# The causal convolution of a Mamba block moved from VectorE to TensorE, in an eight-core Mamba + mixture-of-experts kernel

## What is computed

```python
xn = layernorm(x)
# Mamba branch
z, xBC, dt = split(xn @ in_proj_w)            # 2048 | 2304 | 32
y_conv = conv_b                               # causal depthwise convolution, 4 taps
for k in range(4):
    y_conv = y_conv + xp[:, k:k+L, :] * conv_w[3 - k]
xBC = silu(y_conv)                            # x_part 2048 | B 128 | C 128
state = state * decay + (x_t * dt_t) outer B_t   # scan over tokens, 32 heads of 64
y = state . C_t + x_part * D
g = rmsnorm(y * silu(z)) * norm_w
att = g @ out_proj_w
# MoE branch, every expert computed for every token
ffn = sum_e w_full[:, e] * (xn @ expert_w[e].T)    # 8 experts, top-2 weights
out = x + att + ffn
```

## Time and profile before

| | us |
|---|---|
| median of 2 runs | 1998.78 (1997.82 to 1999.73) |
| the profiled execution | 2002.32 |
| its span (slowest core, core 2) | 2000.8 |
| spans of the eight cores | 1982.9 to 2000.8 |

### The profile page before, as it was taken

How to read it: one execution, slowest core, us unless ns; L and a number is a source line. 1 busy time by engine, 2 the same in 40 slices (tenths; PEclk the granted TensorE clock), 3 DMA queues, 4 the chain that set the end, 5 groups by cost and what they waited for, 6 DMA issues and landing times.

```text
span 2000.8 us, 23963 instructions; the slowest of 8 cores (1982.9 to 2000.8 us)
## 1 busy us (share of the span) xinstructions
PE 1090.3 (54%) x7419; PEld 748.8 (37%) x7419; DVE 1062.4 (53%) x2347; ACT 402.4 (20%) x483; POOL 0.2 (0%) x4
## 2 busy tenths in 40 slices
PE   1111246485757475657665666665576558573400
PEld 1110233363445344544444444543363346342100
DVE  3642474638353845476547645664556454745344
ACT  2354102120122022102220132112111221022200
POOL 0000000000000000000000000000000000000000
PEclk9999988795878688879787887888786779686755
DMA  6852000000000100000010000000100000000077
GB/s 165 283 179 74 27 22 19 22 30 22 22 27 22 45 27 27 22 24 27 27 43 24 30 22 25 25 27 22 48 25 24 19 25 28 27 11 22 11 245 259
DMA packets 64930, 103.62 MB, mean 52 GB/s; under 512 B 8870, under 2 KB 49958, under 8 KB 62246
## 3 DMA queue, kind: packets, MB, share of 16 engines
q1 hardware_dynamic: 60198, 89.51, 14.3%
q10 hardware_dynamic: 4608, 12.58, 1.6%
HBM read 85.28 MB, written 16.78 MB: 51 GB/s over the span
## 4 chain that ended last, share of the span: by engine, by line
PE 35%; DVE 25%; DVEq 9%; issue 8%; ACT 7%; DMA 3%; SPq 1%; ACTq 0%
PE P L639 12%; DVEq L72 8%; PE P L736 6%; PE P L787 6%; PE P L1070 6%; DVE AC L764 6%; DMA OACR<-oaccd 2%; DVE SCR L1017 2%; DVE Y L1012 2%; DVE OACC L660 2%; DVE AC L758 2%; ACT TX L834 2%; DVE AC L845 1%; DVE Y L1023 1%; ACT TZ L799 1%
## 5 line engine op out<-in xcount | busy, mean ns | idle before, releaser
L639 PE MATMUL P<-EWB,XN 128*128 128x256 bf16 x4096 | 581.5, 304 | 195.5 <-DVE EWB L610 108.4
L639 PEld LDWEIGHTS P<-EWB,XN 128*128 128x128 bf16 x4096 | 436.8, 108 | 333.4 <-issue 228.3
L660 DVE SCALAR_TENSOR_TENSOR OACC<-P,WFULL,OACC 128x256 bf16<-128x256 f32 x448 | 213.6, 481 | 376.5 <-PE P L639 356.5
L787 PE MATMUL P<-WIN,XN 128*128 128x512 bf16 x512 | 148.3, 456 | 72.1 <-DVE SZ L822 72.1
L736 PE MATMUL P<-XN,WIN 128*128 128x256 bf16 x1152 | 133.9, 275 | 55.0 <-DVE XB L578 41.1
L764 DVE SCALAR_TENSOR_TENSOR AC<-XB,CW,AC 128x256 bf16<-128x256 bf16 x288 | 139.6, 485 | 22.5 <-issue 1.3
L736 PEld LDWEIGHTS P<-XN,WIN 128*128 128x128 bf16 x1152 | 112.1, 98 | 73.7 <-issue 59.9
L1052 PE MATMUL P<-IBF,Y 128*128 128x128 bf16 x256 | 29.0, 304 | 190.3 <-DVE Y L1026 161.4
L1070 PE MATMUL P<-WOUT,SCR 128*128 128x512 bf16 x512 | 120.9, 397 | 9.2 <-ACT SCR L1059 6.7
L1059 ACT COPY SCR<-P 128x2048 bf16<-128x2048 bf16 x16 | 29.8, 1865 | 465.6 <-PE P L1052 465.6
L787 PEld LDWEIGHTS P<-WIN,XN 128*128 128x128 bf16 x512 | 56.3, 113 | 156.0 <-issue 121.4
(11 more groups left out here) (121 smaller groups left out, 999.1 us busy)
## 6 DMA issues: line engine op xcount, KB each, us to landing
ESTG<-we SPq DMA_DIRECT2D x256, 128.0 KB, 2.1
XR<-x SPq DMA_DIRECT2D x32, 512.0 KB, 5.9
WSTG<-wi SPq DMA_DIRECT2D x8, 1098.0 KB, 7.2
WSTG<-wi SPq DMA_DIRECT2D x8, 1078.0 KB, 8.5
WOSTG<-wo SPq DMA_DIRECT2D x16, 512.0 KB, 4.3
out<-OST ACTq DMA_DIRECT2D x16, 512.0 KB, 5.7
attd<-ATTS ACTq DMA_DIRECT2D x16, 256.0 KB, 2.0
oaccd<-OACC SPq DMA_DIRECT2D x4, 1024.0 KB, 4.5
```

Of the source, the lines that this page charges most:

```text
L639: li = e.matmul(pp4[:, of4:of4 + 256], XN[:, k * L + t * 128:k * L + (t + 1) * 128], EWB[:, eb * 2048 + k * 256:eb * 2048 + (k + 1) * 256] ...
L660: return e.scalar_tensor_tensor(OACC[:, t * 256:(t + 1) * 256], pp4[:, of4:of4 + 256], WFULL[:, t * 8 + ee:t * 8 + ee + 1], OACC[:, t * 25 ...
L787: li = e.matmul(P01[:, bb * 512:(bb + 1) * 512], XN[:, k * L + ch * 128:k * L + (ch + 1) * 128], WIN[:, k * WIN_F + w * 1024 + bb * 512: k ...
```

## The change

- Convolution. Each of the 18 tiles is now four accumulating matmuls of 128x256 on PE. The moving operand is XB shifted by 0 to 3 columns; the weights are four 128x128 diagonal matrices that hold the tap's coefficients. ACT makes the diagonals for every tile anew, by four ACTIVATEs of the identity matrix IBF with a per-partition scale, into a ring of eight (DGS, two tiles). Even tiles accumulate in the second bank of P01, odd tiles in the second bank of P67.
- The result leaves PSUM through ACT: once with the bias to AC, once through tanh with half the bias (CBH, a new constant) to TX. DVE does the two remaining SiLU instructions after every second tile. The separate SiLU waves after the z steps are gone.
- The xBC projections come in nine waves of two tiles, in the first bank of P01. The z steps and the transposes into P01 are halved in width too, so there are twice as many of them.
- The MoE groups rotate over three banks instead of four.
- State update: DVE adds straight from PSUM (P23); YIN and its two ACT copies a chunk are gone. The second half's matmuls wait for the first half's addition.
- The numbers of MoE steps per place (drip) are set anew: 204 in a pair and its two backs, 202 before.

The core of the diff:

```diff
@@ mcbh = st("V", lambda e: e.tensor_scalar_mul(CBH[:], CB[:], 0.5), ...)   (new, once)
-                            sl4 = gi % 4
+                            sl4 = gi % 3
-                            of4 = (sl4 % 2) * 512
+                            of4 = (sl4 % 2) * 512 if sl4 < 2 else 0
-                            if gi >= 4:
-                                ww.append(escq[gi - 4])
+                            if gi >= 3:
+                                ww.append(escq[gi - 3])
...
-                        for wv, (ct0, ctn) in enumerate(
-                                [(0, 4), (4, 4), (8, 4), (12, 4), (16, 2)]):
+                        for wv in range(9):
+                            ct0 = 2 * wv
...
-                            drip(4)
+                            drip(2)
...
+                        cv_ev = [None, None]
+                        mm_cv = {}
...
+                            def dgen(e, ct=ct):
+                                for dd in range(4):
+                                    j = (4 * ct + dd) % 8
+                                    li = e.activation(
+                                        DGS[:, j * 128:(j + 1) * 128],
+                                        IBF[:], AF.Identity,
+                                        scale=CW[:, ct * 4 + dd:ct * 4 + dd + 1])
+                                return li
+                            mdg = st("S", dgen, waits=[mm_cv.get(ct - 2)])
+                            yield
+                            cvp, cvo = (P01, 512) if ct % 2 == 0 else (P67, 512)
+                            def cvmm(e, ct=ct, cvp=cvp, cvo=cvo):
+                                for dd in range(4):
+                                    j = (4 * ct + dd) % 8
+                                    li = e.matmul(
+                                        cvp[:, cvo:cvo + 256],
+                                        DGS[:, j * 128:(j + 1) * 128],
+                                        XB[:, ct * XBW + 4 - dd:
+                                           ct * XBW + 260 - dd],
+                                        start=(dd == 0), stop=(dd == 3))
+                                return li
+                            mm_cv[ct] = st("T", cvmm, waits=[
+                                mdg, wave_ev[ct // 2], cv_ev[ct % 2]])
                             drip(3)
                             yield
+                            def cvev(e, ct=ct, cvp=cvp, cvo=cvo):
+                                e.activation(
+                                    AC[:, ct * 256:(ct + 1) * 256],
+                                    cvp[:, cvo:cvo + 256], AF.Identity,
+                                    scale=1.0, bias=CB[:, ct:ct + 1])
+                                e.drain()
+                                return e.activation(
+                                    TX[:, (ct % 2) * 256:(ct % 2 + 1) * 256],
+                                    cvp[:, cvo:cvo + 256], AF.Tanh, scale=0.5,
+                                    bias=CBH[:, ct:ct + 1])
+                            cv_ev[ct % 2] = st("S", cvev, waits=[
+                                mm_cv[ct], cms.get(ct - 2)])
+                            yield
+                            if ct % 2 == 1:
+                                def comp(e, ct=ct):
+                                    e.tensor_scalar(TX[:], TX[:], 0.5, 0.5,
+                                                    ALU.mult, ALU.add)
+                                    e.drain()
+                                    return e.tensor_tensor(
+                                        AC[:, (ct - 1) * 256:(ct + 1) * 256],
+                                        AC[:, (ct - 1) * 256:(ct + 1) * 256],
+                                        TX[:], ALU.mult)
+                                cm = st("V", comp,
+                                        waits=[cv_ev[0], cv_ev[1]])
+                                cms[ct] = cms[ct - 1] = cm
+                                drip(2)
+                                yield
...
-                        msu = st("T", supd, waits=[st_c23[0], mx])
-                        drip(3)
+                        msu = st("T", supd, waits=[st_c23[0], mx] +
+                                 ([msup] if msup else []))
+                        drip(2)
                         yield
-                        ev = st("S", lambda e, w=w: e.copy(
-                            YIN[:, w * 1024:(w + 1) * 1024], P23[:]),
-                            waits=[msu])
+                        md = st("V", lambda e, c=c, w=w, dto=dto:
+                                e.tensor_tensor(
+                            hx(DTX[:, dto + w * 1024:dto + (w + 1) * 1024], 16),
+                            hx(S_ALL[:, w * 1024:(w + 1) * 1024], 16),
+                            BETB[:, c * 32 + w * 16:c * 32 + (w + 1) * 16]
+                            .to_broadcast([128, 16, HEADDIM]),
+                            ALU.mult), waits=[msu])
+                        drip(1)
+                        yield
+                        msup = st("V", lambda e, w=w, dto=dto: e.tensor_tensor(
+                            S_ALL[:, w * 1024:(w + 1) * 1024],
+                            DTX[:, dto + w * 1024:dto + (w + 1) * 1024],
+                            P23[:], ALU.add), waits=[md], drain=False)
```

More of the change, by code:

```diff
@@ L138, in build_nc @@
         CB = E(nc.sbuf_tensor([128, NXT], F32))
+        CBH = E(nc.sbuf_tensor([128, NXT], F32))
         KCOL = E(nc.sbuf_tensor([128, 2], F32))
@@ L205, in build_nc @@
             ][-1])
+            mcbh = st("V", lambda e: e.tensor_scalar_mul(
+                CBH[:], CB[:], 0.5), waits=[mconst])
             ma1 = st("S", lambda e: e.activation(ROWA[:], ROWA[:], AF.Exp),
@@ L752, in front_gen @@
                             yield
-                        mcv_tiles = []
+                        cv_ev = [None, None]
+                        mm_cv = {}
+                        cm = None
+                        cms = {}
                         for ct in range(NXT):
[L755 to L775, removed]
@@ L792, in zmm @@
                                                 start=(k == 0), stop=(k == NK - 1))
[L793 to L810, removed]
+                                        return li
+                                    mz = st("T", zmm,
+                                            waits=[st_c01[0], m_szprev[0]])
+                                    drip(2)
@@ new lines, in front_gen, with zef @@
+                                    yield
+                                    def zef(e, ch=ch, w=w, bb=bb):
+                                        e.activation(
+                                            TZ[:, bb * 512:(bb + 1) * 512],
+                                            P01[:, 0:512], AF.Tanh, scale=0.5)
+                                        e.drain()
+                                        return e.copy(
+                                            SZ[:, (ch % 2) * D_INNER + w * 1024 + bb * 512:
+                                               (ch % 2) * D_INNER + w * 1024 + (bb + 1) * 512],
+                                            P01[:, 0:512])
@@ L964, in back_gen @@
                     yield
-                    su_ev = []
+                    msup = None
                     msu = None
@@ L998, in back_gen @@
-                    msup = None
-                    for j in range(2):
-                        msup = st("V", lambda e, j=j, dto=dto: e.tensor_tensor(
-                            S_ALL[:, j * 1024:(j + 1) * 1024],
-                            DTX[:, dto + j * 1024:dto + (j + 1) * 1024],
-                            YIN[:, j * 1024:(j + 1) * 1024], ALU.add),
-                            waits=[md] if j == 0 else [], drain=(j == 0))
-                        drip(1)
-                        yield
```

115 lines of the change are left out of this document (50 added, 65 removed).

## The result

The changed kernel took 2010.1 us (median of 43 runs), the kernel before 2004.1 (42 runs, of the same sittings); the ratio is 1.003, with a 95% interval of 1.0019 to 1.004. So it is slower, by 0.3%. The forecast called it a draw, which it is to within 2%, but the sign is wrong, and the draw was made of other parts than I had put into it.

The account below looks back on a forecast made before the run. DVE was taken to bound the convolution and its back, chains of waits the rest. Seven pairs -10.5, first pair -3.5, last back -1: -15 on 2002.3 gives 1987, median 1984, stated 1988; range 1935 to 2050.

Parts of the forecast that it names:

- a draw: Whole kernel: time within 2% (40 us) of before, chance 0.46; faster than 1959 us 0.27, slower than 2039 us 0.27.
- No engine bounds, the loop is serial: Whole kernel: no engine busy above 54%; new convolution loop serial, so DVE's 259 us leave and buy nothing.
- The loop's length: Convolution loop on ACT and PE: 3.28 us a tile at full clock, taken as 3.4, bounds 3.0 and 3.9.
- the two handovers: Convolution loop: 0.15 us from ACT to PE and 0.12 us from PE to ACT in each tile.
- rival 2: Convolution loop with PE at half clock: 3.9 us a tile, +65 us, 2053 us in all; chance 26%.
- rival 1: Convolution loop short, ACT's pointer scale overlapping and clock at 1: 3.0 to 3.1 us a tile, 1942 us; chance 26%.
- The odd chunk's back ahead of the convolution: Convolution stage: back pulled ahead, update matmuls 17.8 us after first projection, PE waiting some 6 us, transposes at 38.4.
- The first pair: First pair's convolution stage: waves 25 us plus tiles 61.2, 86.2 against 89.4, so 3.2 less; whole pair -3.5.
- The halved z steps: z steps: 8.75 us each instead of 7.7, +4.2 for four, less clock given back: +1.2 us a pair.
- State update from PSUM: Even chunk's update: 9.4 to 8.3 us, -1.1, addition at 1.22; with halved transposes and order -2.9 a pair.
- Three banks at nothing: MoE groups on three banks: accumulation 0.5 us after the group, three groups take 2.6, so no cost.
- Rival 3: ACT reloads a table at each change between Identity and Tanh: some 370 us more, 2360 us; chance 2%.

Follow-up runs that it names:

- e2: Changed kernel with the next tile's diagonals made on ACT ahead of this tile's evacuation: ratio 0.927 to the kernel before, 1865 us.
- e1: Changed kernel with two lists of waits turned round, so the convolution's last-arriving waits are named last: ratio 0.986 to the kernel before, 1983 us.
- e4: Changed kernel with two front steps for each step of the odd chunk's back, spreading it over the convolution: ratio 0.986 to the kernel before.
- b3: Kernel before with only the state update added straight from PSUM, convolution still on DVE: ratio 0.992.
- b2: Kernel before with only the MoE groups rotating over three PSUM banks instead of four: ratio 1.003.
- the fastest: Changed kernel with next tile's diagonals ahead of evacuation, waits in arrival order, bias copy moved from ACT to DVE: ratio 0.901 to the kernel before, 1808 us.

## Why the prediction was wrong, point by point

- **No engine bounds, the loop is serial: right.** The same instructions, with one step placed earlier, take 7.6% less (e2). DVE's 232 us (forecast 259 less 17 for the additions) left and bought nothing. ACT is busy for 663.6 us where I had put "near 600"; the prediction's own prices make some 645 (402.4 less 45.3 for SiLU and 32 for YIN's copies, plus 144 tiles of 2.2).
- **The loop's length: the step that failed.** The sum of 3.28 was right for its pieces; e1 shows 3.26. What failed is the term of the two handovers, 0.15 + 0.12, taken from the earlier trace rows, where each instruction waits for one thing only. In the loop they measure 0.35 + 0.20, because of waits named behind the one that arrives last; e1 prices these at 0.26 us a tile. The prediction then went to 3.4 for the clock alone; the mean was 3.69. The 16 tiles of a pair at 0.29 more are 4.6 us, and the stage is 4.9 above before where I had 0.2, or 33 us in seven pairs: this is the miss. With the waits in order (mean 3.43, my 3.4) the kernel is at 0.986, near the forecast (0.995; the sum alone 0.993) and on its side. The bound of 3.9 for a cold loop (rival 2) was not reached; that of 3.0 (rival 1) neither.
- **The odd chunk's back ahead of the convolution: right in its mechanism.** In the pair read the transposes started 40.6 us after the first projections (38.4 forecast), after PE had waited 8.6 us (6 forecast):

```profile
841.40 1.91 PE L739 MATMUL P<-XN,WIN 128*128 128x256 bf16 x16 [1.17 <-DVE XB L728]
...
858.10 0.59 PE L997 MATMUL P<-DTX,BTM 128*128 128x512 bf16 x2
...
882.00 1.86 PE L1068 MATMUL P<-IBF,Y 128*128 128x128 bf16 x16 [8.56 <-DVE Y L1042]
```

  The state update's matmuls come 16.7 us after the projections (17.8 forecast). e4 prices the lost filling at 5 us a pair. (The terms given for the update add up to 8.1, not to 8.3.)
- **The first pair: wrong by 11 us.** I let MoE groups hide two thirds of the copies between the projection waves. There are none yet: the generator's first sixteen steps are loads and casts. The waves come every 4.4 us at half clock, then every 2.8:

```profile
245.21 3.57 PE L739 MATMUL P<-XN,WIN 128*128 128x256 bf16 x16 [0.86 <-ACT XB L750]
249.64 1.91 PE L739 MATMUL P<-XN,WIN 128*128 128x256 bf16 x16 [0.86 <-ACT XB L750]
252.41 1.91 PE L739 MATMUL P<-XN,WIN 128*128 128x256 bf16 x16 [0.86 <-ACT XB L750]
```

  The nine waves take 32 us instead of 25; 18 tiles at more than 3.4 do the rest. The 25 doesn't follow from its terms either: nine waves of 1.75 are 15.8, a third of nine copies with their handovers 2.6, and what the remaining 6.6 are is not said.
- **The halved z steps: wrong sign.** Forecast +1.2, measured -1.8. The price at full clock was about right, a little high: four steps of 8.75 are 35.0 us, and 34.0 were measured. What failed is how much the clock gives back. The four steps took 35.8 us before and would have taken 30.8 at full clock; I had let the shorter gaps give back 3.0 of these 5.0. Seven z windows at 0.95 to 1.00 say that nearly all came back. In the kernel before PE waited 4.7 and 3.4 us ahead of the two slow steps of the earlier trace rows; in the changed kernel's fourth pair its longest wait between z steps is 2.3 us, and all eight halves take 1.89.
- **State update from PSUM: right in the price of the addition, wrong in where it pays.** The addition takes 1216 ns in the profile after, the upper row (1226), and the one-element-a-cycle rule of the Trainium skill's VectorE: DVE Perf Modes (why PSUM operands drop a tier) agrees. The transposes-to-next-pair stretch got 2.5 us shorter (2.9 forecast), but not by the update. That takes 9.36 us from its first matmuls to the epilogue, where it took 9.38 and 8.3 was forecast:

```profile
1011.48 0.59 PE L997 MATMUL P<-DTX,BTM 128*128 128x512 bf16 x2 [2.39 <-DVE DTX L973]
...
1016.49 0.84 PE L997 MATMUL P<-DTX,BTM 128*128 128x512 bf16 x2 [3.54 <-DVE S_ALL L1016]
...
1020.84 0.69 DVE L1028 TENSOR_TENSOR Y<-Y,EC 128x512 bf16<-128x512 bf16 x1
```

  The second half's matmuls now wait for the first addition. In the mean of the even chunks and of eight cores the update takes 10.1 us against 9.8. The 2.5 us are won ahead of it, where the halved transposes and DTX's earlier place stand (1.8 forecast). b3 alone is 0.8% faster; its trace has the odd chunks' update 6 us shorter (27.0 to 20.8) and the convolution stretch 1.8, for which I had forecast nothing.
- **Three banks at nothing:** b2 has 1.003 (1.000 to 1.007), so anything from nothing to 14 us. It may be a share of the loss and cannot be told from none; its trace has a convolution stretch of 93.9 us against 92.4 and a period of 207.7 against 207.0.
- **Rival 3 (tables):** no table load stands in the loop (both kernels have four in all); Identity and Tanh follow each other at 0.54 us.

The sum: six periods at +0.6 are +3.4, the first pair is +7.4, and the eighth pair with what follows it -1.8 (start -0.2). That is +8.8, the difference of the two profiled spans, where -15 was forecast; the ratio gives +6. The misses in a pair are +4.7 (loop), -3.0 (z steps) and +0.4 (the rest), so the loss would have been larger if the z steps had not erred the other way. That the result is still within 2% is in part luck.

## What to carry to other kernels

When work moves to an idle engine, write out who waits for whom in one turn: if the new engine has both the first and the last step of the turn, its idle time is not there to be used until the next turn's first step is issued ahead of this turn's last (7.6% of the changed kernel's time here, with the same instructions). In such a turn, name the wait that arrives last at the end of the list. And measure the parts of a change alone: here parts that gain 1.7% together hid a loss of 2%.

## What the hardware showed that I had not expected

- A wait that has long been satisfied, named behind the one that arrives last, costs about 0.1 us on PE and 0.07 on ACT (handovers of 0.35 with two such waits and of 0.20 with one, against 0.15 and 0.13 in e1; 0.25 on PE where there is only one).
- With PE's work in shorter pieces and shorter gaps the clock was higher: its mean over the span is 0.87 in the changed kernel and 0.89 in the fastest, against 0.81 before. These kernels differ in more than the gaps, so for the span the cause is not shown. The Trainium skill's TensorE: Matmul & The Clock Gate (HAM oscillation) has long idle stretches as what takes the clock down; the z windows agree with that (waits of 3.4 to 4.7 us at 0.84, of at most 2.3 us at 1.00).
- DVE builds a 128x128 bf16 diagonal at a pitch of under 0.2 us (four in 0.74), ACT at 0.3 (four in 1.28).
